# Shift parts of a softmax in the words of the negative maximum, rows placed by four transfers

## The reference

```
scores = q @ k.T * scale          # 128 x 128, from 8 features
attn   = softmax(scores, axis=-1)
out    = attn @ v                 # then all heads @ Wo + bo, added to x
```

## Time and profile before

| what | value |
|---|---|
| three runs | 1085.68, 1090.24, 1093.18 us; median 1090.24 |
| profiled execution, its span | 1087.7 us |
| "heads" steps | about 30 to 370 us of the span |
| "cross" steps | about 740 to 930 us |
| busy: PE, DVE, ACT, POOL | 973.1, 855.0, 692.1, 649.3 us |
| mean granted TensorE clock | 0.958 |

### The profile page before, as it was taken

How to read it: one execution, slowest core, us unless ns; L and a number is a source line. 1 busy time by engine, 2 the same in 40 slices (tenths; PEclk the granted TensorE clock), 3 DMA queues, 4 the chain that set the end, 5 groups by cost and what they waited for, 6 DMA issues and landing times.

```text
span 1087.7 us, 33962 instructions
## 1 busy us (share of the span) xinstructions
PE 973.1 (89%) x10494; PEld 694.1 (64%) x10494; DVE 855.0 (79%) x2398; ACT 692.1 (64%) x1801; POOL 649.3 (60%) x1020
## 2 busy tenths in 40 slices
PE   3699999989998888999998889889999999768997
PEld 2466666656665667777776677665656655556885
DVE  6588899888888778888887888776787877657665
ACT  1377777777776743555665887673666666546775
POOL 8757778877676466640675786168667752323443
PEclk9599999999998979999998999998999999989999
DMA  5776567985666201332332111035555640054551
GB/s 147 181 148 132 116 139 163 185 162 134 143 153 171 74 34 50 98 105 77 106 104 55 37 31 38 26 64 133 115 113 129 130 106 18 6 196 167 194 193 29
DMA packets 81460, 119.69 MB, mean 110 GB/s; under 512 B 16720, under 2 KB 62704, under 8 KB 80288
## 3 DMA queue, kind: packets, MB, share of 16 engines
q1 hardware_dynamic: 66704, 85.24, 32.9%
q0 software_dynamic: 9472, 27.27, 8.2%
q10 hardware_dynamic: 5136, 5.31, 2.5%
HBM read 80.75 MB, written 36.18 MB: 107 GB/s over the span
## 4 chain that ended last, share of the span: by engine, by line
PE 61%; DVE 19%; issue 8%; DMA 5%; ACT 3%; POOL 3%; SPq 1%; DVEq 0%; POOLq 0%; ACTq 0%
PE heads_ps_pv L992 4%; PE heads_ps_max L970 4%; DVE heads_neg_max L770 4%; PE cross_ps_max L960 4%; PE experts_ps_gu L2488 4%; PE cross_ps_max L970 3%; PE cross_ps_pv L992 3%; DMA QK<-heads_qk_parts 2%; PE experts_ps_gu L2490 2%; PE experts_ps_gu L2489 2%; PE heads_ps_out L1054 2%; PE experts_ps_y L2509 2%; PE experts_ps_y L2510 2%; PE experts_ps_hT L2496 1%; PE cross_ps_qk L1316 1%
## 5 line engine op out<-in xcount | busy, mean ns | idle before, releaser
L770 DVE TENSOR_REDUCE heads_neg_max<-heads_ps_max 128x4 f32<-128x512 f32 x256 | 169.5, 681 | 36.0 <-PE heads_ps_max L970 34.4
L844 ACT ACTIVATE heads_E<-heads_ps_exp 128x512 f32<-128x512 f32 x256 | 150.1, 603 | 22.1 <-PE heads_ps_pv L992 17.3
L970 PE MATMUL heads_ps_max<-QK 48*128 48x128 bf16 x1024 | 102.9, 226 | 10.2 <-DMA QK<-heads_qk_parts 5.8
L770 DVE TENSOR_REDUCE cross_neg_max<-cross_ps_max 128x4 f32<-128x512 f32 x128 | 86.2, 682 | 29.5 <-PE cross_ps_max L970 28.9
L974 PE MATMUL heads_ps_exp<-QK 50*128 50x128 bf16 x1024 | 103.0, 222 | 0.0
L2182 POOL DMA_INDIRECT experts_gathered<-experts_y_dram,experts_index x64 | 62.0, 969 | 65.4 <-DMA experts_y_dram<-experts_y_sb 44.1
L844 ACT ACTIVATE cross_E<-cross_ps_exp 128x512 f32<-128x512 f32 x128 | 76.5, 599 | 33.1 <-PE cross_ps_exp L974 17.0
L2404 ACT ACTIVATE experts_act_out<-experts_ps_gu 128x256 f32<-128x256 f32 x110 | 42.3, 384 | 83.0 <-PE experts_ps_gu L2490 82.9
L970 PEld LDWEIGHTS heads_ps_max<-QK 48*128 48x128 bf16 x1024 | 58.9, 97 | 52.2 <-issue 21.0
L1613 POOL TENSOR_TENSOR experts_hidden_lo<-experts_hidden,experts_hidden_hi 128x512 fp32r<-128x512 f32 x32 | 41.4, 1293 | 73.9 <-ACT experts_hidden_hi L1837 66.8
L992 PE MATMUL heads_ps_pv<-heads_E,heads_V 128*32 128x128 f32 x2048 | 84.8, 285 | 0.0
(11 more groups left out here) (325 smaller groups left out, 3173.3 us busy)
## 6 DMA issues: line engine op xcount, KB each, us to landing
experts_share<-experts_cT_dram SPq DMA_DIRECT2D x7, 2304.0 KB, 8.8
heads_qk_parts<-heads_parts POOLq DMA_DIRECT2D x32, 384.0 KB, 4.7
QK<-heads_qk_parts SPq DMA_DIRECT2D x64, 192.0 KB
QK<-heads_qk_parts SPq DMA_DIRECT2D x64, 128.0 KB
cross_qk_parts<-cross_parts POOLq DMA_DIRECT2D x16, 384.0 KB, 4.2
QK<-cross_qk_parts SPq DMA_DIRECT2D x32, 192.0 KB
experts_xs_dram<-load_stats SPq DMA_DIRECT2D x26, 192.0 KB, 3.0
experts_xs<-experts_xs_dram SPq DMA_DIRECT2D x78, 64.0 KB
```

The costliest lines, as they stand in the source:

```text
L770: nc.vector.tensor_reduce(neg_max[:, half, heads.start:heads.stop], ps_max[:, u % 2, :].rearrange("q (h k) -> q h k", h=HU), AX.X, ALU.max ...
L844: nc.scalar.activation(E[:, half, heads.start:heads.stop, :], ps_exp[:, u % 2, :].rearrange("k (h q) -> k h q", h=HU), ACT.Exp, scale=scal ...
L970: last_max = nc.tensor.matmul(ps_max[:, u % 2, i * S:(i + 1) * S], QK[q_of][rows, 0, h, max_of], QK[q_of][rows, 1, h, max_of], start=not m ...
```

## The change

The tile `shift` and the semaphore `shift_hi` go. `neg_max` becomes two buffers in turn. A float32 number's upper 16 bits are a bfloat16 number (its value cut off, not rounded), so the upper half of each word of `neg_max`, seen as bfloat16, serves as the first part where it lies. One VectorE instruction computes the difference between the float32 number and that upper half and writes it, rounded to bfloat16, into the lower half of the same word. The 32 bfloat16 numbers of a query now stand in the order half, head, part. TensorE turns the tile in that order, so the two parts of a half lie on alternate partitions of `shiftT`, and SP places them by four transfers instead of two: 8 source partitions with a step of 2 to one row each. The counts of `shift_placed` double. The first reduction of a batch waits for the transposition two batches earlier (the same buffer) in place of the shift of the batch before.

```diff
-        neg_max = sb("neg_max", [S, HALVES, HH])
-        shift = sb("shift", [S, HALVES, SHIFT, HH], BF16)
+        neg_max = [sb(f"neg_max{p}", [S, HALVES, HH]) for p in range(2)]
...
+        def shift_of(t, ahead):
+
+            return neg_max[(t.k + ahead) % 2][:].rearrange("q a h -> q (a h)").bitcast(BF16).rearrange("q (a h i) -> q a h i", a=HALVES, i=SHIFT)
...
                     for half in range(HALVES):
-                        at = half * BASE + ROWS
-                        sp.dma_start(QK[p][at:at + SHIFT, 0, :, j * S:j * S + S], turned[half * SHIFT * HH:(half + 1) * SHIFT * HH, :]).then_inc(shift_placed[(t.k + MA - 1) % 2], 16)
+                        at, first, last = half * BASE + ROWS, half * SHIFT * HH, (half + 1) * SHIFT * HH
+                        for i in range(SHIFT):
+                            sp.dma_start(QK[p][at + i:at + i + 1, 0, :, j * S:j * S + S], turned[first + i:last:SHIFT, :]).then_inc(shift_placed[(t.k + MA - 1) % 2], 16)
...
                     if u == 0:
-                        need(dve, shift_ready, t.batch(1, MA))
+                        need(dve, shiftT_made, t.batch(1, MA - 1))
...
                     dve.wait_ge(max_taken, t.batch(UNITS, (MA + 1) * UNITS))
-                    need(dve, shiftT_made, t.batch(1, MA))
-                    nc.vector.tensor_copy(shift[:, :, 0, :], neg_max[:]).then_inc(shift_hi, 1)
-                    dve.wait_ge(shift_hi, t.batch(1, MA + 1))
-                    nc.vector.tensor_tensor(shift[:, :, 1, :], neg_max[:], shift[:, :, 0, :], ALU.subtract).then_inc(shift_ready, 1)
+                    low, high = (shift_of(t, MA)[:, :, :, i] for i in range(SHIFT))
+                    nc.vector.tensor_tensor(low, neg_max[(t.k + MA) % 2][:], high, ALU.subtract).then_inc(shift_ready, 1)
...
-                    need(act, shift_placed[q], t.group(32, 32))
+                    need(act, shift_placed[q], t.group(64, 64))
...
-                        pe.wait_ge(shift_placed[t.k % 2], t.group(32, 32))
+                        pe.wait_ge(shift_placed[t.k % 2], t.group(64, 64))
...
-                nc.tensor.transpose(ps_shiftT, shift[:].rearrange("q a i h -> q (a i h)"), identb[:]).then_inc(shiftT_made, 1)
+                nc.tensor.transpose(ps_shiftT, shift_of(t, MA - 1).rearrange("q a h i -> q (a h i)"), identb[:]).then_inc(shiftT_made, 1)
```

More of the change, by code:

```diff
@@ L493, in head_attention @@
         max_taken = sem("max_taken")
-        shift_hi = sem("shift_hi")
         shift_ready = sem("shift_ready")
@@ L767, in maxima @@
                     if u == 0:
-                        need(dve, shift_ready, t.batch(1, MA))
+                        need(dve, shiftT_made, t.batch(1, MA - 1))
                     half, heads = heads_of(u)
-                    nc.vector.tensor_reduce(neg_max[:, half, heads.start:heads.stop], ps_max[:, u % 2, :].rearrange("q (h k) -> q h k", h=HU),
+                    nc.vector.tensor_reduce(neg_max[(t.k + MA) % 2][:, half, heads.start:heads.stop], ps_max[:, u % 2, :].rearrange("q (h k) -> q h k", h=HU),
                                             AX.X, ALU.max, negate=True).then_inc(max_taken, 1)
```

## The result

The changed kernel is slower: 1124.05 us median of four runs (1112.43 to 1134.75) against 1091.71 of four runs of the kernel before; the ratio is 1.027 [1.020, 1.034]. The forecast was 1086, and the range ended at 1101. Run again later, without an edit, it gave 1.043 [1.033, 1.053]; that run is told under the experiments. Where one of them carries an argument, the profile of the later run stands beside it.

The account below looks back on a forecast made before the run. In heads VectorE and TensorE wait for each other once a step, with transfers the next limit; cross is bound by TensorE. Sum: -15.7 + 5.4 + 6.4 = -3.9 us, giving 1086 for the median; range 1072 to 1101.

Parts of the forecast that it names:

- The copy: VectorE, both attention stages: the rounding copy goes, the shift is ready earlier, 15.7 us won (heads 14.2, cross 1.5).
- the lock wins back: Rival: VectorE's new subtraction is stopped by GpSimd as often as the old; +4.8 us, 1095; chance 0.18.
- The issues: SP's queue: four shift transfers a step instead of two, 0.62 us each, every window 1.28 us later.
- the rival of short issues: SP: a transfer to one row costs a window's 0.35 us; -14.3 us, 1076, or 1071 with half the maxima; chance 0.27.
- Just covered, by 0.21: Heads, free pair of steps: the loop through the windows needs 9.36 us with the issues, the pair wants 9.57.
- mean of 0.2 each: 5.4 us: Heads: 27 free groups lose a mean of 0.2 us each to late windows, 5.4 us.
- the spare: Heads: windows landing at 204.97 against the maximum matmul at 206.30, so 1.33 us spare.
- free pair: Heads: two steps, shift issue at 198.24 returning at 208.25, 10.01 us, taken as a case without a wait for windows.
- The 4.5 us: Heads: time taken for a window to land after issue, from the context's transfer on the same queue; other end 6.53.
- SP itself has room: 7.5 us of 10: SP's issues per pair of steps: 2 x (2.56 + 1.19) = 7.5 us of 10.
- the windows decide (slower): Rival: windows land later than the loop allows; landing at 5.5 us gives +14.4 us, 1105; chance 0.17.
- Cross: Cross stage: 1.5 us won from 1.8 us of waits; TensorE full, which covers the added issues.

Follow-up runs that it names:

- e1: New VectorE instruction kept, but shift rows placed by two transfers, each one part for both halves; against the kernel before 0.995, 1086.28 us.
- p1: e1 plus 4 semaphore increments, so that SP spends on the shift what it spent before; against the kernel before 0.990, 1086.54 us.
- x1: Kernel before plus two unneeded transfers between SBUF tiles each step, issued behind the windows; against the kernel before 1.004, 1100.62 us.
- n2: Kernel before plus 21 semaphore increments of SP (1.34 us) ahead of the windows, no added transfer; against the kernel before 1.012, 1109.40 us.
- e2: Kernel before with its old VectorE part, only its two shift transfers cut into four; against the kernel before 1.021, 1119.55 us.
- q1: e1 plus 25 semaphore increments, so that SP spends on the shift what the changed kernel spends; against the kernel before 1.028, 1119.50 us.

## Why the prediction was wrong

**The copy: right, over-sized.** The mechanism and the duration of the new instruction came as put down. The rival by which the lock wins back fell: subtractions of over 0.55 us went from 23 to 7 of 64 (2 in e1), their mean from 342 to 244 ns, and the waits for the shift to 4.5 us in 5. The Trainium skill's rule of a lock between VectorE and GpSimd (page "SBUF — State Buffer", section "SBUF: two separate sides") still agrees with the longest, 699 ns for 179, which ends 34 ns after a GpSimd instruction. Alone, the part gave 1.0% and 0.5% (p1, e1) where 15.7 us, 1.4%, were forecast.

**The issues: right.** 0.62 was taken and 0.635 measured; the rival of short issues fell.

**The step that failed is "Just covered, by 0.21", with its "mean of 0.2 each: 5.4 us".** Three things were wrong in it.

First, the spare. The windows issued until 200.82 are a group's first half (the context's issue follows them), and the matmul at 206.30 is the second batch of the group before, which waits for no windows. By the trace, that group's second half was issued until 195.76, landed at 200.94, and its first matmul stands at 201.36: 0.42 us spare, not 1.33. The next group, of which 200.82 ends the first half, has its last issue until 205.81 and its landing at 212.27, and TensorE waited 0.88 us for it, so the step right behind the "free pair" already waited. The 4.5 us were the landing of another transfer, the context, counted from the start of its issue; windows land a median of 4.48 us after the *end* of theirs, from 3.5 to 6.8, and the median spare over the 32 groups is about 0.75 us. All of this stood in the trace of the kernel before.

Second, SP. "SP itself has room: 7.5 us of 10" counted the shift and the windows, and neither the context nor the experts' weights, 0.35 each, nor windows' issues that stretch (1.90). Measured are 9.28 of 9.76 in a dense pair. The delay itself was well sized, 1.28 forecast and 1.36 measured (4.07 - 2.71), and x1 shows that a busier SP costs little where it delays no windows. So this count was wrong, but the small spare did the harm.

Third, the clock, which was no term of the sum. The rows show TensorE at 4.32 of 7 us while it waits, then a step at 0.57 that takes 7.34 us in place of 4.54, and from 60 us to the end of the maxima 65.0 us at half clock for 6.8. The Trainium skill (page "TensorE: Matmul & The Clock Gate", section "HAM oscillation — how this bites in real kernels") describes a loop in which waits for a transfer let the clock fall, and prices the time at the lower clock as half lost; the rows here agree, with 2.80 us lost in that step's 6.3 us at the lower level, 0.44 of it.

So it was the rival "the windows decide (slower)", with 0.17. Its price, +14.4 us, was about right for the pause alone (n2, 1.2%, 13 us), and less than half of the change's 32 (1124.05 - 1091.71); it had no term for the clock. The sum also takes it that wins and losses add up, and the runs speak against it: 0.990 (p1) and 1.021 (e2) would make 1.011, and the change measures 1.027 and 1.043. With the late windows 1.028 stands against 1.012 (q1, n2). An earlier transposition brings TensorE to the same landing sooner; the windows' waits are 26.3 us in 18 groups against 13.6 in 17, and the time at half clock is 64.9 us against 27.3. That longer waits are what lowers the clock is the reading that fits these numbers; it wasn't tried by itself, and q1 and n2 ran on different chips. Open is also why the changed kernel is 1.027 in its first runs and 1.043 in the later ones.

Cross came nearly as forecast, 177.6 us before and 178.6 and 180.5 after, where 1.5 less was put down; TensorE is full there.

## What to carry to other kernels

Count the issue time of every transfer on an in-order queue, also those that have nothing to do with the edit, and set it against the spare of each landing that stands behind, from that transfer's own landings, not from the median of another; make sure that the landing and the instruction set against each other belong to the same piece of work. Where the granted clock falls after waits, as it did here, a wait that is added to TensorE costs its length and then part of the steps that run at the lower clock, so a loss at the edge can be larger than the missing microseconds. Cut a set of rows so that it takes fewer transfers (by part across both halves, 2 x 0.51 us) and not more (by half and part, 4 x 0.635).

## What the runs showed of the hardware

An issue is paid per transfer, hardly per byte: a 2 KB transfer to one row takes SP 0.635 us, one of 4 KB to two rows together 0.619, and one of 4 KB to two rows 64 partitions apart only 0.510:
```profile
L607 SPq DMA_DIRECT2D QK<-heads_shiftT x128: 495/510/928, 37.6 to 347.6; - x128
```
A semaphore increment on SP takes about 0.06 us in sequence (40 in 2.46 us). VectorE subtracts in place, reading the upper and writing the lower halves of the words that it reads, at the price of an ordinary instruction (179 ns).
